# Statistics that wait for GpSimd's third operation, one normalisation placed in the head, and tail work of the mixers placed a turn sooner

## The reference

```
x = x + attention0(ln(x))      # windows of 16 tokens, 3 heads, bias table
x = x + ffn0(ln(x))            # 96-384-96, signs as weights, clipped by maxima
x = x + attention1(ln(x))      # windows of 64 tokens, 3 heads
x = x + experts1(ln(x))        # 4 experts of 96-384-96, the best 2 of each token
x = x + mixer2(ln(x))          # relu^2, 2-D FFT, block MLP, softshrink, inverse FFT
x = x + experts2(ln(x))
x = x + mixer3(ln(x))          # relu^2, 2-D FFT times routed filters, inverse FFT
x = x + experts3(ln(x))
# ln(v) = (v - mean(v)) / sqrt(var(v) + eps), over the channels
```

## Time and profile before

| | |
|---|---|
| median of 3 runs | 801.93 us (801.03 to 803.57) |
| the profiled execution | 805.04 us |
| its span, first to last instruction | 803.2 us |
| PE busy | 740.7 us (92%) |
| DVE busy | 555.5 us (69%) |
| POOL busy | 560.4 us (70%) |
| ACT busy | 448.2 us (56%) |
| mean granted TensorE clock | 0.953 of full speed |

### The profile page before, as it was taken

How to read it: one execution, slowest core, us unless ns; L and a number is a source line. 1 busy time by engine, 2 the same in 40 slices (tenths; PEclk the granted TensorE clock), 3 DMA queues, 4 the chain that set the end, 5 groups by cost and what they waited for, 6 DMA issues and landing times.

```text
span 803.2 us, 28109 instructions
## 1 busy us (share of the span) xinstructions
PE 740.7 (92%) x10887; PEld 606.8 (76%) x10887; DVE 555.5 (69%) x1579; ACT 448.2 (56%) x817; POOL 560.4 (70%) x879
## 2 busy tenths in 40 slices
PE   4997877899999999989989999999799999999996
PEld 2666666677688888868876788888688877888886
DVE  7687786787566676768874666667968764666655
ACT  4674764576555445387775555454546656454541
POOL 4665556454578877887773978887767676888764
PEclk9697787899999999999999999999979899999999
DMA  7610000021211111000021111110000020111130
GB/s 178 134 13 19 1 1 2 3 52 48 66 53 40 29 29 32 3 1 2 0 51 31 31 32 37 53 31 2 2 2 1 1 60 9 54 33 29 29 91 21
DMA packets 39514, 26.24 MB, mean 33 GB/s; under 512 B 27499, under 2 KB 32348, under 8 KB 39412
## 3 DMA queue, kind: packets, MB, share of 16 engines
q1 hardware_dynamic: 38444, 24.46, 12.0%
q10 hardware_dynamic: 968, 0.38, 0.2%
HBM read 7.92 MB, written 1.57 MB: 12 GB/s over the span
## 4 chain that ended last, share of the span: by engine, by line
PE 70%; DVE 13%; POOL 7%; issue 6%; ACT 4%; POOLq 0%; DVEq 0%; ACTq 0%
PE PS L1865 22%; PE PS L1828 9%; PE PS L1829 8%; PE PS L1832 4%; PE PS L1540 3%; PE PS L1943 2%; PE PS L1956 2%; PE PS L1967 2%; PE PS L1976 2%; POOL H L564 2%; PE PS L1986 1%; PE PS L1653 1%; PE PS L1602 1%; DVE X L1333 1%; PE PS L1840 1%
## 5 line engine op out<-in xcount | busy, mean ns | idle before, releaser
L777 ACT ACTIVATE H<-PS,B 128x512 f32<-128x512 f32 x288 | 175.4, 689 | 157.4 <-PE PS L1832 157.4
L1865 PEld LDWEIGHTS PS<-M,H 128*64 128x64 f32 x4608 | 192.4, 137 | 21.9 <-issue 12.8
L1865 PE MATMUL PS<-M,H 128*64 128x96 f32 x4608 | 205.4, 248 | 1.9 <-DVE X L1333 1.9
L1333 DVE SCALAR_TENSOR_TENSOR X<-PS,G,X 128x96 f32<-128x96 f32 (+1 forms) x384 | 121.7, 318 | 112.5 <-PE PS L1865 102.0
L491 POOL TENSOR_TENSOR msum<-stats 128x4 f32<-128x4 f32 (+1 forms) x60 | 16.6, 276 | 94.4 <-DVE stats L1002 84.1
L1828 PE MATMUL PS<-XH,M1h 128*128 128x512 f32 x192 | 77.1, 401 | 0.0
L1829 PE MATMUL PS<-FHL,M1l 128*128 128x512 f32 x192 | 75.8, 395 | 0.0
L527 POOL TENSOR_TENSOR PF<-G,B 128x1536 f32<-128x1536 f32 x24 | 66.2, 2757 | 10.2 <-DVE G L1324 10.2
L501 POOL TENSOR_TENSOR XN<-X,mean 128x384 f32<-128x384 f32 x55 | 46.3, 842 | 37.4 <-PE PS L1540 37.3
L535 POOL TENSOR_TENSOR ex<-euler,dl 128x16 f32<-128x16 f32 x24 | 69.8, 2908 | 0.3 <-DVE dl L1297 0.2
L505 POOL TENSOR_TENSOR rs<-ve,half 128x4 f32<-128x4 f32 (+1 forms) x60 | 64.6, 1077 | 4.7
(11 more groups left out here) (264 smaller groups left out, 1661.4 us busy)
## 6 DMA issues: line engine op xcount, KB each, us to landing
FHL<-XH SPq DMA_DIRECT2D x36, 192.0 KB, 2.5
FHL<-XL SPq DMA_DIRECT2D x36, 64.0 KB, 2.1
X<-XH SPq DMA_DIRECT2D x12, 192.0 KB, 2.5
raw<-L_ffn_w SPq DMA_DIRECT2D x3, 576.0 KB, 4.9
M<-L_ffn_w SPq DMA_DIRECT2D x3, 576.0 KB, 5.4
XH<-XL SPq DMA_DIRECT2D x24, 64.0 KB, 1.9
out<-X SPq DMA_DIRECT2D x8, 192.0 KB, 2.5
X<-x SPq DMA_DIRECT2D x3, 384.0 KB, 5.8
```

Of the source, the lines that this page charges most:

```text
L777: act.activation(H[p][:, c, :], bank(UB[c]), ACT.Gelu, bias=B1[e][:, c:c + 1]).then_inc(gelu_a, 1)
L1333: ins = dve.scalar_tensor_tensor(xt(g, t), bank(4 + t % 2)[:, e * C:(e + 1) * C], G[:, t, e:e + 1], xt(g, t), ALU.mult, ALU.add)
L1865: ins = pe.matmul(Y[rows, x * C:(x + 1) * C], H[p][:, j, t * P + rows.start:t * P + rows.stop], M2[e][:, j, :], start=c == 0, stop=c == CH ...
```

## The change

Six things change. The statistics wait for POOL's third operation on the former group (`ag_p`, and `fag_p` in `ffn0`) and no longer for its last. Group 2's statistics and normalisation move from turn -1 of the first attention to places ahead of the loop, and POOL's memsets come behind them. The sum `gsum2` and the two memsets of `W1B` and `W2B` move into turn -1 (`weight_rest`), behind the subtraction of the maxima. `expert_weights(2)` moves from the end of turn 5 of `mixer2` into turn 7. The two `whole_gate` of the mixers' tails move from turn 7 to turn 6. SP's first two `stack` of the second expert step come ahead of `low_rows(2)`.

```diff
@@ sync
                 for g in range(2, GROUPS):
                     stack(0, g)
+                for g in range(2):
+                    stack(1, g)
                 low_rows(2)
-                for e in range(1, 3):
-                    for g in range(GROUPS):
-                        stack(e, g)
+                for g in range(2, GROUPS):
+                    stack(1, g)
+                for g in range(GROUPS):
+                    stack(2, g)
@@ gpsimd, attention
-                    if has(g, 3, 2, PREPS[phase]) and not (k == 1 and g == -1):
+                    if has(g, 3, 2, PREPS[phase]) and not (isinstance(g, int) and g == -1):
                         prep(phase, k, g + 3)
@@ gpsimd, ahead of the memsets
             prep(0, 0, 1)
+            prep(0, 0, 2)
@@ scalar, mixer2 (the same move in mixer3, whole_gate(48, 0), to behind routing_relu)
-                if isinstance(g, int) and g == GROUPS - 1:
-                    whole_gate(32, 0)
                 if has(g, 2, 2, PREPS[4]):
                     prep_hi(24 + g + 2, p)
...
                 if has(g, 1):
                     mix_square(g)
+                if isinstance(g, int) and g == GROUPS - 2:
+                    whole_gate(32, 0)
@@ vector, prep_stats and ffn_stats
-                after(dve, xn_p, m)
+                after(dve, ag_p, 6 * m - 5)
...
                 if q == 0:
-                    dve.wait_ge(xn_p, 8)
-                after(dve, fxn_p, q)
+                    dve.wait_ge(ag_p, 6 * 7 + 1)
+                after(dve, fag_p, 6 * q - 5)
@@ vector, head
             halves(WAh[1][0:C], WAl[1][0:C], raw[0:C, 2 * C:4 * C], 2)
+            prep_stats(2, 2, (xin, 16 * 3), None)
...
-            dve.tensor_reduce(gsum2[:, 0:FG], w2t[:, :, 0:FG * gs2].rearrange("p c (g n) -> p g c n", g=FG), AX.XY, ALU.add)\
-               .then_inc(wt_v, 1)
             prep_lo(1, 1)
-            dve.memset(W1B[0:C].bitcast(F32), 0.0)
-            dve.memset(W2B[:], 0.0).then_inc(wt_v, 1)
+
+            def weight_rest():
+                dve.tensor_reduce(gsum2[:, 0:FG], w2t[:, :, 0:FG * gs2].rearrange("p c (g n) -> p g c n", g=FG), AX.XY, ALU.add)\
+                   .then_inc(wt_v, 1)
+                dve.memset(W1B[0:C].bitcast(F32), 0.0)
+                dve.memset(W2B[:], 0.0).then_inc(wt_v, 1)
@@ vector, attention, behind the subtraction
+                    if ka == 0 and isinstance(g, int) and g == -1:
+                        weight_rest()
@@ vector, mixer2
+                if isinstance(g, int) and g == GROUPS - 1:
+                    expert_weights(2)
                 if has(g, 0):
...
                 if has(g, -1):
                     mix_x(0, g - 1, xu[4])
-                if isinstance(g, int) and g == 5:
-                    expert_weights(2)
```

More of the change, by code:

```diff
@@ L923, in mixer3 @@
                     mix_star(g, 0)
-                if isinstance(g, int) and g == GROUPS - 1:
-                    whole_gate(48, 0)
                 if has(g, 2, 2, PREPS[6]):
@@ L937, in mixer3 @@
                     routing_relu(g + 2)
+                if isinstance(g, int) and g == GROUPS - 2:
+                    whole_gate(48, 0)
                 if has(g, 1):
@@ L1180, in body @@
                         ffn_stats(0)
-                    if has(g, 3, 2, PREPS[phase]) and not head:
+                    if has(g, 3, 2, PREPS[phase]) and not (isinstance(g, int) and g == -1):
                         prep_stats(m + 3, g + 3, (prev[0], min(FG, (GT * (g + 3) + GT - 1) // FT + 1)) if ka == 1 and g + 3 < GROUPS else prev, upd)
@@ L1258, in _ @@
                 elif q >= FG - 2:
-                    dve.wait_ge(fxn_p, FG)
+                    dve.wait_ge(fag_p, 6 * FG - 5)
                     prep_stats(8 + q - (FG - 2), q - (FG - 2), (xu[1], q - (FG - 2) + 1), None)
```

## The result

| | before | changed |
|---|---|---|
| median | 801.98 us (800.45 to 805.18, 6 runs) | 793.59 us (792.55 to 798.68, 6 runs) |
| ratio | | 0.9888, interval 0.9864 to 0.9912 |
| the profiled execution, its span | 805.04, 803.2 us | 792.83, 790.9 us |
| mean granted TensorE clock in it | 0.953 | 0.965 |
| PE, DVE, ACT, POOL busy | 740.7, 555.5, 448.2, 560.4 us | 733.9, 554.3, 447.7, 560.5 us |

By the medians the change saves 8.4 us where 6.3 were forecast; the forecast's range holds the result, its middle lies outside the interval (7.1 to 10.9 us).

A forecast was written before the change was run, and what follows sets the result against it. PE, busy 92% of the span, was taken to bound the kernel; 2.76 (head) + 0.78 (into ffn0) + 2.80 (mixer2), about 6.3 us, took the median from 801.93 to 795.6 us, range 791.5 to 799.8.

The forecast's parts named there:

- A, the head's waits: Head of the first attention: PE's waits for the subtraction and for group 2's normalisation shrink by 1.20 and 1.56 us.
- A, the clock: First attention behind the head: the half-rate stretch moves with the work, keeping all 2.76 us; low 1.4, high 6.1.
- rival 1: The clock stays up in the head once both waits go, giving 3.38 us more, 792.2 us; chance 0.25.
- One of the prediction's signs for rival 1: Head: PE ran at clock 1.00 from 11 to 12 us while it was busy.
- its 9.7 us: Head: by the skill's rule, closing both waits also ends the slow stretch, a total saving of 9.7 us instead of 6.3.
- B, into ffn0: Passage into ffn0: without DVE's wait for POOL the last maxima start 0.78 us sooner; low 0, high 1.03.
- The chain from there ... is serial: Into ffn0: from the last maxima, subtraction, exponential and attention's last matmuls follow serially; the gain counted was 0.78 us.
- C, the other statistics: Starts of steps and head: DVE's other waits for POOL are only replaced by slightly later ones, gain 0.
- D, mixer2: Turns 6 and 7 of mixer2: PE's waits for DVE and ACT shrink by 1.73 and 1.07 us, together 2.80.
- E: Turn 7 of mixer3: moving ACT's copy gains 0, as PE's transposes follow POOL; ends 0.6 lost, 0.1 gained.

The follow-up runs named there:

- e8: The changed kernel with the head undone, the statistics' wait and mixer tails as changed: 798.89 us against 803.47 for the kernel before.
- e1: The kernel before with only the statistics' wait changed, nothing moved: 801.42 us against 802.14.
- e9: The changed kernel with group 2's statistics and normalisation back in turn -1: 797.96 us against 803.47 for the kernel before.
- e6: The kernel before, waits unchanged, with 12 extra matmuls for PE in the head's waits: 803.04 us against 802.97.
- e2: The kernel before with only the head's moves, the old statistics' wait kept: 801.31 us against 802.14.
- e5: The kernel before with the head's moves and the new statistics' wait, mixers unchanged: 798.28 us against 802.97.
- e10: The changed kernel with gsum2 and the two memsets back in the head, group 2 early: 797.55 us against 803.47 for the kernel before.
- e7_signs: The changed kernel with ffn0's weight signs on DVE split, three groups ahead of ffn_lo, two after the update of X: 790.25 us against 802.97 before.
- e3: The kernel before with only the mixers' tails and SP's two copies changed: 798.46 us against 802.14.
- e12: The kernel before with only the head's moves and the old wait, timed and profiled a second time: 802.36 us against 802.75.
- e11: The kernel before with head and new statistics' wait, mixers unchanged, timed and profiled a second time: 797.35 us against 803.47.

## Why the prediction was right, and where it was off

**A, the head's waits.** Right in every start: maxima 16.83 (forecast near 16.8), POOL done at 18.65 (18.7), transposes at 20.17 (20.2), 2.81 us against 2.76.

**A, the clock.** The step that failed is "I take it that the fall and the rise move with the work, so that the whole 2.76 us is kept". The clock didn't move with the work, it stayed up: rival 1. Against the profile of before it gave 2.47 us and not 3.38, because turns 0 and 1 at full rate take 26.34 - 20.17 = 6.17 and 6.69 us, not the 5.94 of later turns. The price of the fall differs from profile to profile: from group 2 to group 7 the five profiles with a fall took 31.2 (e8) to 33.6 us (e1), the changed kernel 30.75. e9 shows that the wait ahead of group 2 was enough to bring the clock down, e1 that the first was, e6 that filling PE's waits without shortening them keeps the clock up until PE stops by itself. One of the prediction's signs for rival 1 was misread: at 11 to 12 us PE ran at half rate, whatever the 1.00 in the earlier trace rows says (last section). The rule of the Trainium skill that the prediction weighed (TensorE: Matmul & The Clock Gate, "HAM oscillation — how this bites in real kernels") was right for this place, and its 9.7 us were more than the 8.4 measured. A fall remains possible in an execution with the head, by a stop of PE (e2, e5, e10).

**B, into ffn0.** The mechanism at its start was right, the sum wrong: 0.78 us were forecast, 0.79 arrived at the maxima (64.13 - 58.00 = 6.13, against 5.34 at the scores), and 0.20 were left at PE's last matmuls (72.73 - 67.19 = 5.54). "The chain from there ... is serial" was the faulty step: DVE's `ffn_lo` waits for ACT, which waits for PE, not for the maxima (it came 68.37 - 62.85 = 5.52 us sooner, little more than the scores), and three us of signs and then the update of X stand behind it. e7_signs shows that this was the chain.

**C, the other statistics.** Right: 0. e1 and the table of waits show the wait replaced by others.

**D, mixer2.** 2.80 forecast, 2.83 in the changed kernel, 2.82 in e3. **E.** 0, and 0: in turn 7 of `mixer3` PE starts 0.10 us behind POOL, as before.

**A part of the profiles' difference that isn't shown to be the change's.** Between the first transposes inside `mixer3` and the first inside the third expert step the profile of before took 99.39 us, the changed one 95.41. The 99.4 us, with a turn at half rate as in the earlier trace rows, stand also in the profiles of e2 and e5, while the other eleven have 95.4 to 96.3, among them e12, which has e2's very program, and e1 and e6 without the moves in the mixers. So the program alone doesn't decide it. But the three profiles with it stand among the seven without the moves in the mixers, and none of the seven with them has it: that the moves make it rarer, e3's second rival, is neither shown nor excluded. Without these 3.98 us the two profiles differ by 8.2, near the medians' 8.4.

**What stays open.** By the medians the head alone gave 0.8 and 0.4 us, the wait 0.7, both together 4.7 and 6.1. In the first attention the profiles show no mechanism by which the two need each other (e12 against e11: 0.4 us); in `ffn0` and behind it the head with the old wait took 2 us longer in both profiles, at a lower granted clock, which has no cause shown, and between other kernels' profiles (e7 aside) the same stretch differs by 5 us, from 101.50 (e10) to 106.55 (e3); and the intervals allow for sums that fit. Whether executions with a stop or a fall are truly rarer with the new wait, or in the whole change, wasn't settled.

## What to carry to other kernels

A large wait of an engine on the page may be worth nothing (17.8 us of DVE's here), while 3 us on PE's own path, twice, are worth their full length: go by what the bounding engine waits for at each place. Where PE's waits are closed ahead of a dense stretch, price the clock in that stretch as a term of its own, from turns at either level in the trace. Behind a wait that is removed, follow every engine's queue up to the next point at which PE waits; in `ffn0` the next one stood 3 us further on, and moving work out of its way gave more than the change's own edit there.

## What the runs showed of the hardware that was not expected

PE can stop for 0.89 to 2.23 us between two matmuls of one group, with no wait in the program. It does so at fixed places: after 3 of 16 matmuls of turn 0 (e5, e10) and after 53 of 96 of turn 1 (e2, e10); in e6, with 12 matmuls more ahead, after 41. All lie between 25 and 36 us. The traces also hold the transfers of instructions; from the page of e10_early, part 3 (packets, MB, share):

```profile
q8 instruction: 69, 1.13, 0.6%
```

These packets have 16,384 bytes each. Their times stand beside PE's at the two places (in e6 at the one after 41):

| profile, turn | packet starts | lands | PE goes on | behind the landing |
|---|---|---|---|---|
| e5, turn 0: stop | 24.55 | 25.50 | 26.91 | 1.41 |
| e10, turn 0: stop | 25.32 | 26.20 | 27.68 | 1.48 |
| e2, turn 1: stop | 30.52 | 31.45 | 32.94 | 1.49 |
| e10, turn 1: stop | 32.45 | 33.81 | 35.28 | 1.47 |
| e6, turn 1: stop | 32.50 | 33.84 | 35.16 | 1.32 |
| changed, turn 0 | 21.84 | 23.10 | 25.48 | 2.38 |
| changed, turn 1 | 27.39 | 28.34 | 31.55 | 3.21 |
| before, turn 0 | 25.46 | 26.38 | 29.67 | 3.29 |

In none of the 14 profiles does PE pass one of these places less than 1.25 us behind the landing of the packet, and in all five stops it goes on 1.3 to 1.5 us behind it. So a stop comes where PE is at the place before its instructions are. That the queue is PE's is read from this fit, and no run tested it. The transfers in the stops are no longer (0.88 to 1.36 us) than those without one in the table (0.92 to 1.26); what is late is their start, and why it varies is open. In the kernel before PE comes to the place of turn 0 only at 29.67, long behind the packet: the head, by bringing the work there to 25.5 us, also brings PE within reach of this wait.

The Trainium skill (Runtime: NRT & Kernel Launch, "Instruction fetch mechanics") says that instruction memory is refilled in blocks of 16 KiB, 256 instructions, by a DMA queue that the engine's sequencer drives. The traces agree in the size of the packets, and in the distance of the places: between the two lie 124 matmuls, each with its weight load, which are 248 instructions, and with some ten waits between them that would be, as an estimate, one block.

The granted clock of the profile can't be read in the first 14 us. It says 1.00 there in all 14 profiles, but the first record of the clock in the traces begins only at 14.50 us (before) to 17.44 us (e12), and the matmuls say otherwise. PE's timeline before, neighbouring matmuls of 512 columns at three times:

```profile
12.11 0.63 PE L1526 MATMUL PS<-XH,WAh 97*96 97x512 f32 x1
12.54 0.63 PE L1527 MATMUL PS<-XL,WAh 96*96 96x512 f32 x1
...
26.04 0.63 PE L1527 MATMUL PS<-XL,WAh 96*96 96x512 f32 x1
26.47 0.63 PE L1528 MATMUL PS<-XH,WAl 97*96 97x512 f32 x1
...
40.79 0.39 PE L1527 MATMUL PS<-XL,WAh 96*96 96x512 f32 x1
41.02 0.39 PE L1528 MATMUL PS<-XH,WAl 97*96 97x512 f32 x1
```

The starts are 0.43 us apart at 12 us, as at 26 us where the clock is at 0.50, and 0.23 us at 40.8 us where it is at 1.00. So PE begins this kernel at half rate, and the level rises only between 14 and 18 us.
